# Layer-norm statistics by two ScalarE passes in place of VectorE's, and new instruction orders, in a two-layer transformer kernel

## What is computed

```python
x = _layernorm(x + _L0_attn_ref(x, w_project, w_out))
x = _layernorm(x + _L0_ffn_ref(x, gate_w, up_w, down_w, gate_s, up_s, down_s))
x = _layernorm(x + _L1_attn_ref(x, Wq, bq, Wk, bk, Wv, bv, Wo, bo))
x = _layernorm(x + _L1_ffn_ref(x, W_up, W_gate, W_down))

def _layernorm(x, axis=-1, eps=1e-05):
    m = jnp.mean(x, axis=axis, keepdims=True)
    v = jnp.var(x, axis=axis, keepdims=True)
    return (x - m) / jnp.sqrt(v + eps)
```

## Time and profile before

| | us |
|---|---|
| median of 3 runs | 263.96 (262.76 to 265.11) |
| profiled execution, its own time | 265.93 |
| its span, first to last instruction | 264.0 |
| mean granted clock of TensorE | 0.983 |
| PE busy | 245.5 (93%) |
| DVE busy | 200.4 (76%) |
| POOL busy | 179.4 (68%) |
| ACT busy | 162.5 (62%) |

### The profile page before, as it was taken

The page is one execution under the profiler, slowest core; times in us unless marked ns, Lnnn a source line. Parts: engine busy times, 40 slices in busy tenths (PEclk is TensorE's granted clock), DMA queues, the critical chain, the costliest instruction groups (busy, mean ns, idle before and its releaser), DMA issues.

```text
span 264.0 us, 6802 instructions
## 1 busy us (share of the span) xinstructions
PE 245.5 (93%) x2438; PEld 217.3 (82%) x2438; DVE 200.4 (76%) x593; ACT 162.5 (62%) x292; POOL 179.4 (68%) x238
## 2 busy tenths in 40 slices
PE   8688997998999999899999899898999999999990
PEld 8677995677788989789999899585769888999980
DVE  2567796499968638977998699699999857847563
ACT  4662536568795884574543497838594597644543
POOL 8736356598673589897876665878764785737363
PEclk9999997699999999999999999999999999999998
DMA  6969974075324333265006405626000001000102
GB/s 163 297 172 260 239 194 133 12 219 147 118 82 142 101 88 114 80 195 166 2 15 176 130 3 148 176 73 174 2 2 4 1 4 40 2 0 4 40 0 79
DMA packets 23312, 26.39 MB, mean 100 GB/s; under 512 B 3184, under 2 KB 18288, under 8 KB 23280
## 3 DMA queue, kind: packets, MB, share of 16 engines
q1 hardware_dynamic: 23136, 25.71, 34.9%
q10 hardware_dynamic: 144, 0.26, 0.3%
HBM read 12.20 MB, written 1.05 MB: 50 GB/s over the span
## 4 chain that ended last, share of the span: by engine, by line
PE 55%; SPq 9%; ACT 9%; POOL 8%; DVE 6%; issue 6%; DMA 6%; POOLq 0%; ACTq 0%; DVEq 0%
SPq L523 8%; PE psum L715 6%; PE psum L716 6%; PE psum L551 6%; PE psum L552 5%; PE psum L553 5%; PE psum L660 5%; PE psum L642 5%; ACT probs L821 3%; PE psum L739 2%; PE psum L620 2%; PE psum L740 2%; DMA raw<-a 2%; PE psum L663 2%; DMA k_stack<-k_part 2%
## 5 line engine op out<-in xcount | busy, mean ns | idle before, releaser
L821 ACT ACTIVATE probs<-psum 128x768 f32<-128x768 f32 x64 | 49.4, 810 | 12.3 <-PE psum L644 7.6
L1178 POOL TENSOR_SCALAR_AFFINE_SELECT probs<-probs 128x512 f32<-128x512 f32 x64 | 42.9, 682 | 18.7 <-ACT probs L821 18.0
L1200 POOL TENSOR_TENSOR hidden<-hf,hidden 128x512 fp32r<-128x512 f32 x28 | 36.9, 1319 | 24.4 <-ACT hidden L867 24.4
L978 DVE TENSOR_REDUCE block_max<-psum 128x6 f32<-128x768 f32 x32 | 28.5, 940 | 9.8 <-PE psum L616 9.8
L1070 DVE SCALAR_TENSOR_TENSOR hf<-th,psum 128x512 f32<-128x512 f32 x28 | 19.2, 686 | 16.9 <-ACT th L859 11.9
L642 PE MATMUL psum<-q_stack,k_stack 98*128 98x256 bf16 x128 | 27.6, 286 | 4.3 <-ACT probs L821 1.4
L989 DVE CUSTOM_DVE_ANT_0 masked<-psum,mask 128x256 bf16<-128x256 f32 x64 | 26.5, 414 | 3.9 <-PE psum L621 3.9
L551 PE MATMUL psum<-xT_hi,gu_hi 128*128 128x256 f32 x88 | 25.7, 292 | 0.0
L644 PE MATMUL psum<-q_stack,k_stack 98*128 98x128 bf16 x128 | 24.9, 227 | 0.0
L552 PE MATMUL psum<-xT_lo,gu_hi 128*128 128x256 f32 x88 | 24.9, 283 | 0.0
L553 PE MATMUL psum<-xT_hi,gu_lo 128*128 128x256 f32 x88 | 24.9, 283 | 0.0
(11 more groups left out here) (159 smaller groups left out, 903.2 us busy)
## 6 DMA issues: line engine op xcount, KB each, us to landing
q_stack<-q_part SPq DMA_DIRECT2D x48, 128.0 KB, 2.5
k_stack<-k_part SPq DMA_DIRECT2D x48, 128.0 KB, 2.5
raw<-f SPq DMA_DIRECT2D x24, 256.0 KB, 2.7
raw<-a SPq DMA_DIRECT2D x8, 256.0 KB, 4.2
raw<-f0gu SPq DMA_DIRECT2D x4, 352.0 KB, 4.2
x<-x_nat SPq DMA_DIRECT2D x4, 256.0 KB, 6.0
raw<-f0dn SPq DMA_DIRECT2D x3, 256.0 KB, 2.7
out<-x SPq DMA_DIRECT2D x3, 256.0 KB, 2.3
```

Source lines behind the costliest of these rows:

```text
L821: nc.scalar.activation(probs[(n - 1) % 4][:, :, :], place(key)[:, :, 0:T + P], ACT.Exp, scale=SC).then_inc(exp_done, 1)
L978: nc.vector.tensor_reduce(block_max[b % 2][:, 2 * i:2 * i + 2, 1:4], both(key)[:, :, 0:3 * P].rearrange("p j (c t) -> p j c t", t=P), mybi ...
L1178: pool.affine_select(out=diag, in_=diag, compare_op=ALU.is_ge, fill=0.0, base=0, pattern=[[0, 2], [0, 2], [1, P]], channel_multiplier=-1). ...
L1200: pool.tensor_tensor(hidden[(n - 1) % NHID][1][:, :, :], hf[n % 2][:, :].rearrange("p (a t) -> p a t", a=2), hidden[(n - 1) % NHID][0][:, ...
```

## The change

Three things change together.

First, the statistics. VectorE adds both halves of a residual (256 tokens) in one instruction, and no longer runs bn_stats and bn_aggr. ScalarE has a new step SM (and MT:130, MT:131 for the last layer norm's halves): for each half a Copy of `res` scaled by -1/(D sqrt D), whose accumulator gives minus the mean over sqrt D, then a Square of res / sqrt D with that as the bias, whose accumulator gives the variance. Their full outputs go to the place in x that the normalization then overwrites.

Second, POOL multiplies by sqrt D instead of -1 to get the offset, with the same number of instructions.

Third, all five orders and the table of banks are new.

```diff
+            def moments(n, b, halves):
+                k_ = n % 2
+                for tt in halves:
+                    act.wait_ge(res_done, 2 * n - 1 + tt)
+                    nc.scalar.activation(x[:, TT * b + tt, :], res[k_][:, tt, :], ACT.Copy, scale=-1.0 / (D * D ** 0.5),
+                                         accum_out=mv[k_][:, tt, 0:1]).then_inc(mean_done, 1)
+                for tt in halves:
+                    act.wait_ge(mean_done, 2 * n - 1 + tt)
+                    nc.scalar.activation(x[:, TT * b + tt, :], res[k_][:, tt, :], ACT.Square, scale=1.0 / D ** 0.5,
+                                         bias=mv[k_][:, tt, 0:1], accum_out=mv[k_][:, tt, 1:2]).then_inc(var_done, 1)
...
+                if step == "SM":
+                    moments(nth("LN", l, b), b, range(TT))
+                if step == "MT":
+                    moments(NLN, b, (i,))
...
-                for tt in halves:
-                    if gain_ap is None:
-                        ins = nc.vector.tensor_tensor(res[k_][:, tt, :], o[:, tt, :], x[:, TT * b + tt, :], ALU.add)
-                    else:
-                        ins = nc.vector.scalar_tensor_tensor(res[k_][:, tt, :], o[:, tt, :], gain_ap, x[:, TT * b + tt, :],
-                                                             ALU.mult, ALU.add)
-                    ins.then_inc(res_done, 1)
-                for tt in halves:
-                    dve.wait_ge(res_done, 2 * n - 1 + tt)
-                    nc.vector.bn_stats(stats[k_][:, tt, :], res[k_][:, tt, :]).then_inc(stats_done, 1)
-                for tt in halves:
-                    dve.wait_ge(stats_done, 2 * n - 1 + tt)
-                    nc.vector.bn_aggr(mv[k_][:, tt, :], stats[k_][:, tt, :]).then_inc(var_done, 1)
+                xs = x[:, TT * b + halves.start:TT * b + halves.stop, :]
+                if gain_ap is None:
+                    ins = nc.vector.tensor_tensor(res[k_][:, halves, :], o[:, halves, :], xs, ALU.add)
+                else:
+                    ins = nc.vector.scalar_tensor_tensor(res[k_][:, halves, :], o[:, halves, :], gain_ap, xs, ALU.mult, ALU.add)
+                ins.then_inc(res_done, halves.stop - halves.start)
...
-                pool.tensor_tensor(offset[k_][:, c], mv[k_][:, c, 0], minus_one[:, c], ALU.mult)
+                pool.tensor_tensor(offset[k_][:, c], mv[k_][:, c, 0], root_d[:, c], ALU.mult)
...
 TENSOR_STEPS = """
-    QK:000-1 XI:010 XI:020 XI:030 V:000 QK:010-1 V:010 S:000-7 QK:020-1 QK:030 MX:000 S:010-3 QK:031 S:014-6
-    V:020 S:017 S:020-2 ST:000-4 S:023 MX:010 PV:000 ST:005-6 PV:001 ST:007 S:024-5 PV:002 ST:010-1 PV:003
+    QK:000 XI:010 QK:001 XI:020 QK:010-1 V:000 V:010 V:020 XI:030 QK:020 S:000-3 QK:021 S:004-5 QK:030-1 S:006-7
+    MX:000 S:010-7 ST:000-6 MX:010 PV:000-1 S:020-3 PV:002 S:024-5 ST:007 ST:010-3 PV:003 ST:014 V:030 PV:010-1
```

123 lines of the change are left out of this document (61 added, 62 removed), and 14 rows, old and new, of the table BANKS.

## The result

The changed kernel took 268.06 us (median of 6 runs, 265.8 to 270.02) against 263.92 (6 runs, 262.76 to 265.11): a ratio of 1.0141 [1.0101, 1.0182]. So it is slower by 4 us, where 2.8 us less were forecast, and it lies outside the range of 257.0 to 267.0. The ratio leaves out one slow run of the six, 270.02 us.

A forecast was written before the change was run, and what follows sets the result against it. PE was taken as the bound, its idle time and a clock fall as the reservoir. Start -4.2, VectorE's relief -1.5, ScalarE's passes +2.0 and tail +0.9 summed to -2.8 us: 261.2 us, range 257.0 to 267.0.

The forecast's parts named there:

- new orders (the start): Start of the kernel: reordered DMAs and PE steps give PE a lead and a better clock, 4.2 us gained.
- relief of VectorE: Statistics and shorter adds off VectorE, some 17.9 us less busy, worth 1.5 us where it is tight (0 to 4).
- ScalarE's passes and tail: PE waits from a fuller ScalarE in 64 to 101 and 195 to 222 us, +2.0, and the tail, +0.9.
- lead 2.4 us: Start: first transposed scores near 38 us instead of 42.2, less three score steps not yet done, 2.4 us gained.
- rival B: The start's lead is absorbed by the next wait: start 1.5, VectorE 1, against 2.0 and 0.9, 264.4 us; chance 0.24.
- a fall of the clock: Granted clock 0.50 from 43.7 to 50.1 us, expected to go or shorten: 1.8 us gained (0 to 3.2).
- what would make it wrong: A stacking wait returning, or the clock falling at another thin place, such as 32 to 38 us.
- sum of 37.4: ScalarE in 64 to 101 us: 28.57 us busy plus four layer norms of 2.2 makes 37.4 of 37, so full.
- that latency lies beside other batches' PE work: Layer norm chain 1.2 us later plus ScalarE's queue, taken as hidden for 14 of the 16.
- The tail: After the last matmul, add, passes, normalize and store end later: +0.9 us (0.5 to 1.5).
- A: Rival: ScalarE becomes the bound in 64 to 101 and 195 to 222 us, 5.5 us of PE waits, about 267.5; chance 0.20.
- D: Rival: Square isn't in the loaded table, two loads of 1283 ns per layer norm, some +25 us; chance 0.01.

The follow-up runs named there:

- new_order_old_stats: Changed kernel's orders and banks without the steps SM and MT, with the old kernel's adds, bn_stats and bn_aggr on VectorE: 266.42 us, 1.0115 to the old kernel.
- after_cheap_stats: Changed kernel with each of the 64 statistics passes on ScalarE over 16 columns instead of 256, part of the reduction left out: 263.12 us, ratio 0.9995.
- after_again: Changed kernel run once more unedited, for a second trace and the clock of each run: 266.99 us, ratio 1.0134 to the kernel before.
- before_again: Kernel before the change run once more unedited, for a second trace and the clock of each run: ratio 1.0018, profiled span 261.8 us.
- cheap_plus_load: after_cheap_stats plus three copies of 32 columns on ScalarE behind each normalization, which nobody waits for: 265.5 us, ratio 1.0050 to the kernel before.
- before_cheap_stats: Kernel before the change with bn_stats over 16 of 256 columns, most of the reduction left out, orders as they were: 264.02 us, ratio 0.9982.
- after_warm: Changed kernel with 16 unread products of ones on PE ahead of the wait for batch 0's row maxima: 268.06 us, 1.0196 to the kernel before.
- before_warm: Kernel before the change with unread products of ones, nine ahead of the first scores, six ahead of the first transposed scores: 264.65 us, ratio 1.0052.

## Why the prediction was wrong

Split by the runs (differences of their ratios, of 264 us), the change reads so. The measured column is new_order_old_stats (1.0115 - 1), after_cheap_stats less that (0.9995 - 1.0115, with the short passes still on ScalarE, so the relief itself is a little more), and after_again less after_cheap_stats (1.0134 - 0.9995), which holds the tail too. The first carries 1.0 us of noise either way, the other two 1.3:

```
term                       forecast   measured
new orders (the start)       -4.2      +3.0
relief of VectorE            -1.5      -3.2
ScalarE's passes and tail    +2.9      +3.7
sum                          -2.8      +3.5
```

*The steps that failed are the start, taken as a gain of 4.2 us, and the new orders behind it, taken at nothing.* The start's times by hand were right: first scores 19.34 (19.3), maxT_lo at 33.2 to 33.6 (33), first transposed scores 38.83 (38). What was wrong is the step from there to "lead 2.4 us", and what was left out behind it. Three things were in it. First, PE's work that is passed over isn't gone: in after_again the first transposed scores come 2.9 us earlier than in before_again (39.76 against 42.64), and the first residual's add 1.7 us later (63.15 against 61.41, with one step of transposed scores more ahead of it); from 50 to 62 us PE is busy 10.28 of 12 there and 10.86 in before_again, and its waits name VectorE's maxima and ScalarE's exp, which keep their pace whatever PE's lead is. The best point to compare is D:000, the first down product, ahead of which PE has the same steps in both orders. It starts at 87.31 and 85.39 us in the two traces of before, at 86.17, 87.17 and 86.37 in those of after, after_again and new_order_old_stats: nothing of the lead is left. That is what rival B said, with 1.5 us of gain left over that weren't there.

Second, 1.8 us were taken for a fall of the clock that was seen in one execution, and one whose time stood 2.0 us above the median; the new orders have their own fall at 32 to 36 in its place, which the text named as what would make it wrong, and in all runs a mean clock of 0.983 against 0.990.

Third, the other orders in the middle were costed at nothing beyond the relief. From D:000 to the end it is 176.7 and 176.4 us in the traces of before and 180.1 in that of new_order_old_stats, so most of the loss stands behind the start (that trace is of a run 2.0 us above its median, with a fall of the clock to 0.57 at 166 to 170 us, so that the 3.5 us between them are more than the orders cost). PE is busy 182.83 of 190 in the middle there against 186.78 in before_again, and its longest wait in layer 1 is for VectorE's row maxima (1.3 us in four pieces). One place shows in every trace: from 60 to 72 us PE is busy 10.0 to 10.8 us of 12 in the eleven with the new orders and start of after, whichever their statistics, and 11.3 to 12.0 in the five with the old orders and VectorE's statistics. Its waits there name VectorE's maxima and the DMA of the joined ones (0.8 and 0.7 us in after_again). How the 3.0 us divide between clock and waits isn't settled: the share of low clock allows up to 1.3 us of it (3.9 us against 2.6).

*ScalarE's passes.* The mechanism was right and its size half right. A Copy pass is 0.40 us from start to start and a Square 0.49 (forecast 0.55 on average, bounds 0.49 and 0.71), a layer norm 1.8 us (2.2). But I costed them as load on a full engine, and over the stretch named ScalarE wasn't full: 33.37 of 37 us. The sum of 37.4 counted four layer norms in 64 to 101 us; in the new orders the fourth add comes at 102.32 (after_again). In pieces of 6 us ScalarE does come to 5.82 (78 to 84 us, after_again), and PE is full there. Most of the price came by way of the chain, as far as the runs tell: add, four passes, four instructions on GpSimd, normalization, each queue standing still for the other. I had the part before GpSimd 1.2 us longer and wrote that for 14 of 16 "that latency lies beside other batches' PE work"; the whole is 0.9 us longer (4.64 against 3.72) and PE does wait for what stands behind it. Of the 3.7 us the load makes about 1.5 by cheap_plus_load (0.2 to 2.7 by the intervals); that the rest is chain is what remains, not a measurement of its own. The tail is in it: +0.7 us there, forecast +0.9, right.

*VectorE's relief.* 1.5 us was forecast; it is nothing that can be told in the old orders (before_cheap_stats) and 3.2 in the new ones (1.9 to 4.5 by the intervals). Here the relief had no price of its own apart from the order in which it was used.

*The rivals.* A had the mechanism and nearly the time: 267.5 for a measured 268.1, but through load in two stretches, and with a start of 2.0 to 4.2 us kept. B had the mechanism of the start. That the orders cost 3.0 us instead of gaining less stood in no case, so that A's total came within 0.6 us of the measured one is in part luck. D is out: ScalarE's groups show no table load more than before. The rule of the Trainium skill ("ScalarE: Activation LUTs", Rules for kernel authors) that plain arithmetic belongs on VectorE came out right here, with 0.89 us for a half tile on ScalarE (0.40 + 0.49) against 0.59 on VectorE. The estimate worked out from the same page's figures (What ACT_TABLE_LOAD costs), 0.40 and 0.49 us for passes without and with an operand for each partition, agrees with the traces (409 and 497 ns).

## What to carry to other kernels

Before moving work to an idle engine, follow the chain that the work stands in, not only the engine's busy time: every queue that hands it on waits for the whole chain, and in the tightly ordered kernel here 0.5 us of GpSimd's part in each of 16 chains was worth 2.4 us (1.0 to 3.8 by the intervals), while 12 us less on ScalarE with the chain as long as before were worth little that could be told. A lead of PE at one point is worth something only if no paced engine stands before the next common point: compare the time at which the stage ends, not at which it begins. When products are put in to fill a wait, look in the trace whether they ran in it: those of after_warm didn't. And never take a gain from a feature of one profiled execution before a second one shows it.

## What was not expected of the hardware

The granted clock differs from run to run of one kernel with nothing changed (0.980 to 0.997 for before over the 17 runs beside after_again), and its fall in the start isn't always at the same place: 43.7 to 50.1 us in one trace of before, 22 to 27 in the next. With products in PE's idle time before_warm had a clock of 0.994 on average (row below from 22 to 27 us) and no gain in time; in after_warm the clock was at 0.57 while such products ran.

```profile
22.00:27.00 5.00, 4.66 (x57) 4.00 (x55) 5.00 (x7) 1.57 (x2) 3.30 (x2) 1.00 1.09 246
```

A pass of ScalarE keeps half of its price or more when it is short: Copy is 207 ns for 16 columns and 409 for 256, Square with its bias 295 and 497. The read of the accumulator that follows each pass is 190 ns, of which all but 0.09 us lies under its neighbours. And a power of two numbers a partition on GpSimd is 0.69 us, half of its chain of 1.4.
